# Attention with paged keys on one core: sample 6's heads 4 and 5 turned by DMA, the second queries' root groups ahead of the fourth mask, and the first turn's GpSimd and ScalarE work in another order

## The reference

```python
q = _rope(_rmsnorm(x @ Wq.T, q_norm_w), pos)      # 32 query heads of 128
k = _rope(_rmsnorm(x @ Wk.T, k_norm_w), pos)      # 8 key heads of 128
v = x @ Wv.T
k_all = concat([k_cache[block_table], k])         # 512 cached keys and 128 new ones
v_all = concat([v_cache[block_table], v])
scores = where(valid, q @ k_all.T * D ** -0.5, -1e30)
x = x + (softmax(scores) @ v_all) @ Wo.T
```

## Time and profile before

| what | value |
|---|---|
| median of 3 runs | 1277.1 us (1275.13 to 1280.2) |
| the profiled execution | 1275.63 us, its span 1273.9 us |
| busy share of the span | PE 99%, PE weight loads 84%, VectorE 72%, GpSimd 65%, ScalarE 62% |
| granted TensorE clock | 1.00 throughout |
| first score of the attention, last stretch begins | 286.79 us, 1238.89 us |

### The profile page before, as it was taken

One profiled execution on the slowest core, in us unless ns is written; L12 is line 12 of the kernel. 1 busy time (PEld: TensorE's weight loads), 2 busy tenths in 40 slices (PEclk: granted clock), 3 DMA queues, 4 the chain that ended last, 5 costly groups with the idle time before them and its releaser, 6 DMA issues.

```text
span 1273.9 us, 25215 instructions
## 1 busy us (share of the span) xinstructions
PE 1257.2 (99%) x6553; PEld 1076.1 (84%) x6553; DVE 913.3 (72%) x2658; ACT 785.6 (62%) x1850; POOL 826.7 (65%) x810
## 2 busy tenths in 40 slices
PE   9999999998999999999999999999999999999998
PEld 8888877877888888888888888888888888888886
DVE  6532357778877777887777788777777887777774
ACT  5731333637666668676666676766667767666664
POOL 2110011338778888687888887877887869788863
PEclk9999999999999999999999999999999999999999
DMA  8321224277667678755676787567777775667744
GB/s 290 115 83 38 84 71 142 60 262 211 126 132 160 148 142 228 189 130 129 145 157 153 157 223 193 128 136 146 161 159 201 170 199 128 135 155 151 156 101 83
DMA packets 356912, 190.41 MB, mean 149 GB/s; under 512 B 302402, under 2 KB 321218, under 8 KB 356546
## 3 DMA queue, kind: packets, MB, share of 16 engines
q1 hardware_dynamic: 337824, 136.32, 46.1%
q10 hardware_dynamic: 11410, 33.69, 8.1%
q0 software_dynamic: 7568, 19.14, 6.7%
HBM read 119.71 MB, written 16.91 MB: 107 GB/s over the span
## 4 chain that ended last, share of the span: by engine, by line
PE 86%; DVE 6%; issue 4%; DMA 3%; ACT 2%; ACTq 0%; POOL 0%; DVEq 0%; POOLq 0%
PE bank L1697 18%; PE tail L1737 14%; PE wide L1767 14%; PE tail L1804 13%; PE wide L464 4%; PE wide L544 3%; PE bank L1720 3%; PE wide L1731 3%; PE bank L464 3%; PE tail L464 3%; PE wide L599 2%; DMA spread<-one_over_denominators 1%; PE bank L544 1%; PE bank L599 1%; DVE tail L2270 1%
## 5 line engine op out<-in xcount | busy, mean ns | idle before, releaser
L1737 PE MATMUL tail<-prT,vt 128*128 128x512 f32 (+1 forms) x975 | 251.0, 400 | 0.2
L1737 PEld LDWEIGHTS tail<-prT,vt 128*128 128x128 f32 x975 | 173.1, 189 | 36.3 <-DVE prT L2221 5.2
L1804 PE MATMUL tail<-woT,oT 128*128 128x512 f32 x768 | 179.6, 390 | 0.9 <-DVE oT L2274 0.9
L1804 PEld LDWEIGHTS tail<-woT,oT 128*128 128x128 f32 x768 | 144.1, 188 | 31.1 <-DVE oT L2274 1.3
L1767 PE MATMUL wide<-kT,qT 128*128 128x320 f32 x512 | 159.4, 311 | 2.0 <-DVE mx L2250 1.7
L1767 PE MATMUL wide<-kT_low,qT 128*128 128x320 f32 x512 | 158.3, 309 | 0.0
L1767 PE MATMUL wide<-kT,qT_low 128*128 128x320 f32 x512 | 158.1, 309 | 0.0
L1354 POOL TENSOR_TENSOR tick<-tick 128x1 f32<-128x1 f32 x255 | 53.1, 208 | 154.9 <-DMA turned<-parts 47.1
L1993 ACT ACTIVATE raw<-raw,nm,q_scale 128x640 f32<-128x640 f32 x124 | 114.6, 925 | 61.1 <-DVE nm L2253 59.0
L1412 POOL TENSOR_TENSOR parts<-raw,parts 128x1280 f16<-128x1280 f32 x55 | 145.7, 2649 | 8.0
L2250 DVE CUSTOM_DVE_ANT_0 raw<-wide,bias 128x640 f32<-128x640 f32 x124 | 101.7, 820 | 27.4 <-issue 26.9
(11 more groups left out here) (308 smaller groups left out, 3040.2 us busy)
## 6 DMA issues: line engine op xcount, KB each, us to landing
w_ring<-pair_weights SPq DMA_DIRECT2D x80, 256.0 KB, 4.3
k_raw<-k_pages SPq DMA_DIRECT2D x512, 32.0 KB, 1.8
v_raw<-v_pages SPq DMA_DIRECT2D x512, 32.0 KB, 2.7
spread<-one_over_denominators ACTq DMA_DIRECT2D x32, 512.0 KB, 4.2
xTb<-x_transposed ACTq DMA_DIRECT2D x31, 512.0 KB, 3.9
rope<-rope_tables SPq DMA_DIRECT2D x31, 256.0 KB, 3.3
out<-y POOLq DMA_DIRECT2D x31, 256.0 KB, 4.3
w_raw<-w_gate_up SPq DMA_DIRECT2D x10, 512.0 KB, 3.5
```

The costliest lines, as they stand in the source:

```text
L1737: last = nc.tensor.matmul(tail[g][:, first * S:end * S], vt[v_part][:, j, g * D:(g + 1) * D], prT[p_part][:, first:end, j, :], start=(j == ...
L1804: last = nc.tensor.matmul(place[:, :], oT[:, g, o_part, (h % REP) * S:(h % REP + 1) * S], woT[w_part][:, h, :], start=(h == o_part == w_pa ...
```

## The change

- `THIRDS` is 2 to 6 instead of 2 to 5: heads 4 and 5 of sample 6 are turned by DMA too, in every pair. SP issues these two turnings, in pairs 0 to 2, behind five of the next pair's weight chunks, and then three more chunks and sample 7's values.
- The weight chunks 12 to 15 are loaded after the next pair's first values instead of before.
- In late turns DVE does the root's four groups after the first three masks (one, one and two groups) instead of after the first four, and `normalise(1)` after the fourth mask instead of the first. ACT's `copy_values(1)` stands after the fifth exponential instead of the first.
- First turn: GpSimd instead of DVE takes the rests of heads 0 and 1; its weight rests are split over three places; ACT copies the turned heads 0 and 1 one step later; the denominators are spread after the copies of queries and keys, not before.
- `halve` of heads 2 and 3 waits until both groups of the sample before are normalised (outside the first turn).

```diff
@@ -1280,7 +1280,7 @@
-    THIRDS = range(2, 6)
+    THIRDS = range(2, 7)
...
@@ -1399,6 +1398,8 @@
             pool.wait_ge(s_exp, u * HP + HALF * (k + 1))
+            if k and not first_turn:
+                pool.wait_ge(s_norm, u * G)
             carry(n)
...
@@ -1477,7 +1478,7 @@
                 pool.wait_ge(s_step, u * NSTEP + MASKED)
-                halve(u, before, n, 0, True, False)
+                halve(u, before, n, 0, True, True)
...
@@ -1491,6 +1492,8 @@
                 halve(u, before, n + 2, 1, False, then_x is not None and extra != "next")
+                if left:
+                    low_weights(own, left[1], NCHUNK)
                 if has_third(b):
...
@@ -1502,11 +1505,10 @@
             if first_turn:
-                low_weights(own, 3 * KT, 4 * KT)
+                low_weights(own, 3 * KT, LEFT[0])
                 pool.wait_ge(s_init[1], 16 * BLK)
-                low_weights(own, 4 * KT, LEFT[0])
-
-        LEFT = (NCHUNK - 2, NCHUNK)
+
+        LEFT = (4 * KT - 1, NCHUNK - 2)
...
@@ -1629,17 +1630,20 @@
+        WEIGHTS_FIRST = 5
...
                 turn_probs(pair, B - 2)
-                load_weights(pair + 1, 0, NRING)
+                load_weights(pair + 1, 0, WEIGHTS_FIRST)
+                turn_third(pair, B - 2)
+                load_weights(pair + 1, WEIGHTS_FIRST, NRING)
                 load_values(pair, B - 1, pages)
...
                 load_keys(pair + 1, 0, pages, KEYS_FIRST)
-                load_weights(pair + 1, 3 * KT, 4 * KT)
                 load_values(pair + 1, 0, pages)
-                load_weights(pair + 1, 4 * KT, NCHUNK)
+                load_weights(pair + 1, 3 * KT, NCHUNK)
...
@@ -2050,6 +2052,8 @@
                 squares(1, 0, REP)
                 if back and not share:
+                    high_turned(u, before_back, 0, True)
+                if back and not share:
...
@@ -2072,11 +2076,12 @@
-            if back and not third:
+            spread_late = front and (third or not share)
+            if back and not spread_late:
                 spread_shares()
             early(1)
...
@@ -2085,8 +2090,9 @@
                 high(0, 3, kT[:, :, L:NK], bank[0][:, 0:G * S].rearrange("p (g c) -> p g c", g=G))
+            if back and spread_late:
+                spread_shares()
             if third:
-                spread_shares()
                 high_turned_third()
...
@@ -2112,7 +2118,7 @@
-                    if back and h == 0:
+                    if back and h == (REP if second_queries_late(pair, b, front, back) else 0):
                         copy_values(1)
...
-                high_turned(n, before_front, 0, not back)
+                if back:
+                    high_turned(n, before_front, 0, False)
...
@@ -2331,13 +2338,14 @@
                 for h in range(HP):
+                    if late and h == 0:
+                        dve.wait_ge(c_free[1], before[1] + 3 + FIRST)
                     mask_max(h)
-                    if back and h == 0:
+                    if back and h == (3 if late else 0):
                         normalise(1)
-                    if late and h < 4:
-                        if h == 0:
-                            dve.wait_ge(c_free[1], before[1] + 3 + FIRST)
-                        next(second_root, None)
+                    if late:
+                        for _ in range((1, 1, 2)[h] if h < 3 else 0):
+                            next(second_root, None)
...
-                    if not back and h == HALF + 1:
-                        for i in range(HALF):
-                            rest_of(i)
```

More of the change, by code:

```diff
@@ L1318, in turns @@
                 turn(pair, last + 3, before(last + (pair * B + 3)), True, True, True, None, True, True)
-            turn(pair, 6, before(pair * B + 6), True, True, True, None, True, True)
             more = pair + 1 < NPAIR
@@ L1516, in run @@
             LOOP = BEGUN + CARRIES + 1
-            SIXTH = LOOP + THIRD_CARRIES * (len(THIRDS) - 1)
-            SEVENTH = SIXTH + CARRIES + 1
+            SEVENTH = LOOP + THIRD_CARRIES * (len(THIRDS) - 1)
+            AFTER = SEVENTH + CARRIES + 1
             def middle(pair):
@@ L1523, in middle @@
                     turn(pair, b + 3, b * THIRD_CARRIES + (pair * NCARRY + LOOP), b + 1, b + 4)
-                turn(pair, 6, pair * NCARRY + SIXTH, 4, 7)
             with pool.Fori(0, NPAIR - 1) as pair:
@@ L1528, in run @@
                 turn(pair, B - 1, pair * NCARRY + SEVENTH, B - 3, 0, "next")
-                turn(pair + 1, 0, pair * NCARRY + (SEVENTH + CARRIES), B - 2, 1)
-                turn(pair + 1, 1, pair * NCARRY + (SEVENTH + 2 * CARRIES), B - 1, 2, "out")
+                turn(pair + 1, 0, pair * NCARRY + AFTER, B - 2, 1)
+                turn(pair + 1, 1, pair * NCARRY + (AFTER + CARRIES), B - 1, 2, "out")
             pair = NPAIR - 1
@@ L1533, in run @@
             turn(pair, B - 1, pair * NCARRY + SEVENTH, B - 3, None)
-            n = pair * NCARRY + (SEVENTH + CARRIES)
+            n = pair * NCARRY + AFTER
             add_share(NPAIR * B - 2, B - 2, n)
@@ L1635, in run @@
                 load_unit(7, pair, 2)
-                with sp.Fori(0, len(THIRDS)) as b:
+                with sp.Fori(0, len(THIRDS) - 1) as b:
                     load_unit(2, pair, b + 3)
@@ L1661, in run @@
                 load_unit(5, NPAIR - 1, b + 3)
-            load_unit(9, NPAIR - 1, B - 1)
             turn_probs(NPAIR - 1, B - 1)
@@ L2074, in turn @@
                 if third and ahead:
-                    load_x(b + 1)
+                    load_x((b + 1) % B if isinstance(b, int) else b + 1)
             early(0)
```

## The result

The changed kernel takes 1285.8 us in the median of five runs (1282.4 to 1288.2), against 1277.1 (1274.9 to 1280.2): a ratio of 1.0063, 95% interval 1.0038 to 1.0089. The interval lies above 1, so the change makes the kernel slower, by 0.6%. I had forecast 1273.6. Its profiled execution has a span of 1283.9 us, 10.0 more than before; 1270.4 was forecast, so 13.5 us are to be explained.

What follows compares the result with a forecast made beforehand. TensorE, busy end to end, bounds the kernel except at waits in late and first turns. Terms -4.0 - 1.0 - 1.2 + 3.9 - 1.2 = -3.5 us took the median from 1277.1 to 1273.6, whole range 1268 to 1279.

Steps and rivals of the forecast that it cites:

- Root groups: Four late stretches: root ends 1.6 us earlier, removing 1.0 of 1.22 us each; -4.0 us, bounds 0 and -4.9.
- chunks 12 to 15: Stretches 533.43 and 1024.68: moving these weight chunks behind the values takes away 0.77 and 0.23 us; -1.0, bounds 0 and -1.0.
- Sample 6, last pair: Last pair, where no weights follow: sample 6 becomes like samples 2 to 5; -1.2 us.
- First turn: First turn: of two TensorE waits totalling 2.66 us, -1.2 us counted, bounds -0.4 and -2.7.
- Sample 6 in pairs 0 to 2: Heads 4 and 5 by DMA feed DVE late through GpSimd, TensorE 1.3 us later per pair; +3.9, bounds -3.6 and +5.
- 5.55 us more: GpSimd's added work per pair for sample 6: 4.17 us on `pr_third` plus 1.38 us for the low copy.
- 1.7 us later: Turn 7: DVE starts its four rests this much later, since GpSimd's idle time absorbs only 3.56 us of added work.
- Rival 5: DVE rests and GpSimd copies exclude each other, 1.25 us more in three pairs: +3.75, 1277.3 us; chance 0.08.
- SP's two turnings take 3.07 us: SP's queue in sample 6: issue time of the two turnings, delaying sample 7's 16 value DMAs from 982.11 to 985.9.
- So this costs nothing more while that 1.0 us lasts: Sample 7: later values delay DVE's masks to 1003.8, still 1.0 us before GpSimd's parts are there, so no added cost.
- the wait that I had forecast, before the keys' transposes: Sample 7, pairs 0 to 2: TensorE waits for late DVE, idle 1 to 2 us, going on 1.3 us later.
- values too late: Sample 7's values land late and delay DVE through ACT's group copy: +10.5 us over three pairs, 1284.1; chance 0.12.

Runs made afterwards that it cites:

- root_only: Kernel before with only the root groups ahead of the fourth mask and the ACT and GpSimd moves belonging to it: span 1274.7 us, ratio 0.9997 to before.
- last_six: Changed kernel, but sample 6's heads 4 and 5 go by DMA in the last pair alone: span 1270.0 us, ratio 0.9962 to before.
- experiments 1 to 3: Three edits of the changed kernel around GpSimd's store (1.0043, 1.0026, 1.0035 of before); kernel before with that store moved (1.0129); the latter with a slower bias form (1.0005).
- (a): Changed kernel, GpSimd waiting for DVE's bias before its store and six weight rests in sample 7's turn: span 1276.1 us, ratio 1.0043 to before.
- (c): Changed kernel, with each of weight rests 3 to 7 waiting for the one before to complete: span 1276.3 us, ratio 1.0035 to before.
- experiment 6: Store behind rests, ACT's values cast behind its group 1 copy, chunk casts 8 to 11 later; five or three chunks ahead of the turning: 1.0013, 1.0028 of before.
- Experiment 3: Kernel before with the store right ahead of the rests, and the bias also writing a sum (slower form): span 1276.3 us, ratio 1.0005 to before.
- values_cast_later: Changed kernel, store behind the rests, ACT's values cast behind its group 1 copy, casts of chunks 8 to 11 later: span 1281.8 us, ratio 1.0013.
- weights_three: Changed kernel, store behind the rests, three weight chunks instead of five ahead of the third turning: span 1278.1 us, ratio 1.0050 to before.
- (b): Changed kernel, with GpSimd's accumulating store issued behind the six weight rests in sample 7's turn: span 1277.3 us, ratio 1.0026 to before.

## Why the prediction was wrong

*Root groups* (-4.0) and *chunks 12 to 15* (-1.0): right in direction, mis-sized. The four late stretches gave 3.0 us together. In the one that shows the root alone, 779.50, it was 0.44 where I counted 1.0. The fourth mask has all four groups ahead of it and not three, as I wrote: it began 6.85 us after the stretch's first score (791.32), where the rows before had 6.45 and I had 6.7. The 0.1 to 0.2 us that I left for the fourth mask's buffer measured 0.33 (a step of 0.56 us for 0.23), and a wait of 0.3 us five microseconds on, for ACT's squares of a bank that TensorE wants (L1949), was not in the sum at all. The chunks are worth 0.8 us in one pair by `root_only`, and nothing in its others.

*Sample 6, last pair* (-1.2): measured -1.3, and -1.1 in `last_six`. *First turn* (-1.2): -1.4 in the profiled run, +0.3 to -1.3 in others by the one wait shown above. The hold for the spread was in the prediction as a bound (-0.4), and `last_six` lay 0.7 us beyond it; the other eleven profiles with this part lie at -0.8 to -1.4.

*Sample 6 in pairs 0 to 2* (+3.9) is where it failed, by three steps.

1. GpSimd has "5.55 us more", and DVE starts its rests "1.7 us later". That was all that I let GpSimd's new order do to DVE. I moved GpSimd's store past the splitting of the keys, up to the weight rests, and looked only at when each queue comes to each instruction. What the store does to an instruction of another engine was not asked. It cost 4.2 and 4.1 us in two pairs of the profiled run (37.5 against 33.3), shown by experiments 1 to 3. Before, DVE met the same rests with 0.49 to 1.62 us. Rival 5 had the right two engines and the wrong instructions: it was priced on the four rests of `raw`, each against one copy of parts, at 1.25 us a pair.
2. "SP's two turnings take 3.07 us." They took 6.2 to 7.1 in pairs 0 to 2, behind five chunks of 256 KB and an x of 512 KB; I took the price from a place without the chunks, and one on the low side (2.8 to 4.2 us in samples 3 to 5 of the kernel before). TensorE then waits in sample 6, where I had it at 29.9 us: 0.8 to 1.8 us a pair, in a term that was nil.
3. "So this costs nothing more while that 1.0 us lasts." In pair 1 ACT's cast of the values came when I said it would (forecast 35.4 us after sample 6's first score, measured 35.6; 35.9 to 36.8 in (a) to (c)), and the copy of group 1 ended 0.6 us later than I said. But I compared the masks only with GpSimd's parts. TensorE wants the fifth mask's buffer itself, and waited 0.83 us for it at 761.14. Behind it the wait that I had forecast, before the keys' transposes, was there with 0.39 us, since TensorE came late already. Where experiment 6 took the first away, pair 1's 6 + 7 were 63.6 us; my forecast for a pair was 63.5.

So in pair 1, which had no stall, 6 + 7 came to 64.0 instead of 63.5. That this is near is partly luck: sample 6 was 0.8 us over and sample 7 0.3 under. The rivals: values too late was real, but an addition and not an alternative. I gave slower 0.15 and wrote that "cases of both signs are small"; the sum had one term with four queues, GpSimd's, SP's, ACT's and DVE's, moved at once, and its bounds of -3.6 to +5 took in only lateness.

One reading of the prediction was wrong as well. It took DVE's merged row of four rests, 3.91 us, as 0.98 us each, and said that neither engine held the other. One by one they are (view of the line, in pair 2 of the kernel before):

```profile
L2234 DVE TENSOR_TENSOR parts<-raw,parts x4: 811/811/1707, 1003.1 to 1006.2; 128x640 f16<-128x640 f32 x4
```

The first took 1.71 us and ended at 1004.80, 0.69 us after GpSimd's copy (1002.86 + 1.25 = 1004.11); the others took 0.81. So the copy did hold the rest, until the copy's end: rival 5's mechanism was in the rows already. It did not make the miss: in pair 1 of the changed kernel the four take 4.4 us (762.91 to 767.30), in the kernel before 3.9 in pair 2 and 4.3 in pair 1.

The bias's 7.48 us bears on the same rule. The Trainium skill (SBUF — State Buffer, Who interferes with whom) says that `tensor_scalar` can take a mode in which VectorE uses the pair of ports it shares with GpSimd, that the form which also writes its accumulator does not, and that the second to come is blocked for the whole of the other's instruction. Experiment 3 agrees with the first two: 0.74 us always, against 0.48 or up to 7.49. The last fits DVE's rest above, and the bias where no store is ahead (0.47 to 1.65 us), but does not go far enough behind the store: there DVE waited for six instructions.

Why the store's issue makes the difference, no run here shows, nor whether another DMA issued by GpSimd would do the same. GpSimd's rests of `wq0T` differ, though (view of their line, in stretch 469.19 to 537.90 of the changed kernel, then in pair 2 of the kernel before):

```profile
L1370 POOL TENSOR_TENSOR wq0T<-w_ring,wq0T x4: 1512/1533/1575, 500.9 to 504.7; 128x512 fp32r<-128x512 f32 x4
```

```profile
L1371 POOL TENSOR_TENSOR wq0T<-w_ring,wq0T x4: 1302/1310/1487, 992.9 to 996.9; 128x512 fp32r<-128x512 f32 x4
```

In both they start 1.25 us apart (but for the one of 1.49, which met the bias). Behind the store each is recorded as some 1.53 us long, so it overlaps the next by 0.3 us; before, by 0.05. DVE does not cause this: in (a) all six are 1.57 to 1.61 us long with the bias long done. In (c) the first behind the store is 1.59 to 1.61, and those behind a pause are 1.29 to 1.31 again. That a rest is taken up before the last has given the ports back fits all of this, and is only argued.

## What to carry to other kernels

When a change moves an instruction in one engine's queue, list what the other engines run beside its new neighbours, and not only who waits for it; in this kernel the store's issue right ahead of a run of GpSimd's operations had to be kept off from a fast one-input operation of VectorE that others wait for. Before you call a mechanism absent, look at a merged row one instruction at a time. Price a transfer from a place with the same transfers ahead of it. When a wait is hidden by a margin, measure the margin against every reader of what comes late, TensorE's buffers too; and where a saving of 1.2 us needs four queues moved, take it first where nothing competes, as in the last pair.

## What was not expected of the hardware

- A DVE operation of 0.48 us took up to 7.49 us beside six GpSimd operations of 1.3 us behind a store; without the store ahead of them no more than 1.65, and with an accumulator written 0.74 in all 32 places.
- Two transposing DMAs issued behind five 256 KB loads held SP's queue for 6.2 to 8.4 us and landed up to 15.7 us after issue (981.77 to 997.47 in `values_cast_later`), against 2.8 to 4.2 us and a landing 3.4 to 5.2 us after issue in samples 3 to 5 of the kernel before.
- A wait of 4.8 us brought the granted clock of a stretch to 0.95 and 1.6 us of slower matmuls behind it, a third on top of the wait. Shorter ones did too: in `weights_three` two waits of 1.01 and 0.84 us, 1.3 us apart, stood ahead of a fall that left the stretch (469.86 to 503.58) at 0.95; one of 2.05 us in (b) left 1.00.
- A VectorE operation with two inputs (`parts<-raw,parts`) took 1.71 us instead of 0.81 beside one GpSimd copy of 1.25 us.
